# Feed-forward of a fused attention block as four f16 products on exact ternary weights, moved behind the block scores

## The reference

```
x = L0_attn_h                                                   # (2, 1024, 256)
x = _layernorm(x + _L0_attn_ref(x, ...))                        # 16 heads of 128, window of 64 + compressed blocks of 16
x = _layernorm(x + _L0_ffn_ref(x, weight, bias))

def _L0_ffn_ref(x, weight, bias):
    scale = jnp.mean(jnp.abs(weight))
    w_t = jnp.clip(jnp.round(weight / (scale + EPS)), -1.0, 1.0)
    w_ste = weight + jax.lax.stop_gradient(w_t * scale - weight)
    return jnp.einsum('bsi,oi->bso', x, w_ste) + bias
```

## Time and profile before

| | |
|---|---|
| median of 3 runs | 435.04 us (433.79 to 436.04) |
| profiled execution, its own time | 433.26 us |
| its span in the trace | 431.3 us (2.0 us lie around it) |
| mean granted TensorE clock | 0.966 of full speed |
| steps with a feed-forward and attention | i = 2 to 15, each 19.6 to 22.1 us |
| tail without attention | i = 16 and 17, from 405.2 us to the end |

### The profile page before, as it was taken

The page is one execution under the profiler, slowest core; times in us unless marked ns, Lnnn a source line. Parts: engine busy times, 40 slices in busy tenths (PEclk is TensorE's granted clock), DMA queues, the critical chain, the costliest instruction groups (busy, mean ns, idle before and its releaser), DMA issues.

```text
span 431.3 us, 8663 instructions
## 1 busy us (share of the span) xinstructions
PE 374.5 (87%) x3111; PEld 305.3 (71%) x3111; DVE 339.8 (79%) x679; ACT 275.1 (64%) x802; POOL 302.6 (70%) x190
## 2 busy tenths in 40 slices
PE   6996798688898999999898999898999999888782
PEld 5994586476676868687877786776777687767671
DVE  3686798859989999998898889999898998952411
ACT  3558845948584957667676757685958595846100
POOL 1836180538777897979797969797978888776705
PEclk9998999969999999999999999999999999999785
DMA  7992006688768597859584767685776858492330
GB/s 249 300 268 94 1 0 99 247 241 100 123 76 134 98 139 96 123 109 124 99 116 91 105 108 109 112 112 108 101 130 82 145 87 133 87 126 47 56 55 24
DMA packets 148235, 50.19 MB, mean 116 GB/s; under 512 B 136545, under 2 KB 146785, under 8 KB 147937
## 3 DMA queue, kind: packets, MB, share of 16 engines
q1 hardware_dynamic: 147376, 49.31, 64.4%
q10 hardware_dynamic: 816, 0.33, 0.3%
HBM read 11.87 MB, written 4.19 MB: 37 GB/s over the span
## 4 chain that ended last, share of the span: by engine, by line
PE 30%; DVE 20%; ACT 17%; POOL 14%; issue 11%; DMA 4%; SPq 1%; POOLq 0%; ACTq 0%; DVEq 0%
ACT room_h L816 12%; PE PS L658 8%; POOL ao L1191 6%; PE PS L609 4%; PE PS L576 4%; DVE room_wg L1090 3%; DVE ao L1090 3%; PE PS L637 3%; PE PS L427 3%; PE PS L629 3%; POOL room_wo L1235 3%; DMA aoT<-ao 2%; DVE room_K L1039 2%; DVE room_K L1104 2%; PE PS L467 2%
## 5 line engine op out<-in xcount | busy, mean ns | idle before, releaser
L1191 POOL TENSOR_TENSOR ao<-room_wg,ao 128x1024 f16<-128x1024 f32 x32 | 68.2, 2133 | 24.8 <-ACT ao L698 17.8
L658 PE MATMUL PS<-V,room_wg 128*128 128x129 f32 x512 | 69.9, 288 | 14.9 <-ACT room_h L816 8.9
L658 PEld LDWEIGHTS PS<-V,room_wg 128*128 128x128 f32 x512 | 64.7, 200 | 20.7 <-ACT room_h L816 11.3
L1201 POOL TENSOR_TENSOR room_wg<-room_comp,keep 128x1024 f32<-128x1024 f32 x32 | 74.7, 2356 | 2.0 <-ACT room_comp L807 2.0
L816 ACT ACTIVATE room_h<-PS,room_K 128x8 f32<-128x8 f32 (+7 forms) x256 | 70.4, 361 | 2.6 <-DVE room_K L1039 2.3
L816 ACT ACTIVATION_READ_ACCUMULATOR room_h<-PS,room_K 128x1 f32 x256 | 61.8, 247 | 0.0
L629 PE MATMUL PS<-Weff,aoT 128*128 128x256 f16 x512 | 58.5, 273 | 2.5 <-DMA aoT<-ao 2.4
L1207 POOL TENSOR_TENSOR ny<-nx,nu 128x16 f32<-128x16 f32 x16 | 46.8, 2923 | 18.4 <-DVE nx L1012 18.3
L629 PEld LDWEIGHTS PS<-Weff,aoT 128*128 128x128 f16 x512 | 48.9, 97 | 8.5 <-issue 2.6
L576 PE MATMUL PS<-room_h,kT 128*128 128x512 f16 x192 | 46.3, 379 | 6.9 <-DVE room_wg L1090 6.6
L803 ACT ACTIVATE room_comp<-PS 128x512 f32<-128x512 f32 x64 | 37.4, 599 | 16.1 <-PE PS L576 15.9
(11 more groups left out here) (178 smaller groups left out, 759.5 us busy)
## 6 DMA issues: line engine op xcount, KB each, us to landing
H<-in_L_attn_h SPq DMA_DIRECT2D x4, 512.0 KB, 6.3
room_wg<-in_L_attn_Wg SPq DMA_DIRECT2D x1, 2048.0 KB, 12.6
cw_rows<-staged SPq DMA_DIRECT2D x1, 2048.0 KB, 6.4
CW<-cw_rows SPq DMA_DIRECT2D x1, 2048.0 KB, 7.9
out<-room_wo SPq DMA_DIRECT2D x16, 128.0 KB, 2.6
CW<-in_L_attn_Wq_up SPq DMA_DIRECT2D x2, 512.0 KB, 12.5
room_wo<-in_L_attn_Wo SPq DMA_DIRECT2D x1, 1024.0 KB, 13.8
room_h<-room_K SPq DMA_TRANSPOSE x64, 3.2
```

What stands on the lines that cost most here:

```text
L658: last = nc.tensor.matmul(pv, Pm[:, c, 2 * pr:2 * pr + 2, :], V[:, 2 * i + c, :], start=True, stop=True)
L1191: G.tensor_tensor(ao16[:, 1, :, c, :], ao[:, c, :, :], ao16[:, 0, :, c, :], ALU.subtract).then_inc(g_al, 1)
L1201: G.tensor_tensor(Pm[:, c, :, :], E[:, c, :, :], keep[:, :, :], ALU.mult).then_inc(g_mask, 1)
```

## The change

The feed-forward's weight stays ternary (-1, 0, 1) in f16, which holds it exactly; `x1` is split into an f16 high part and an f16 rest, so the product becomes four f16 matmuls (two parts, two halves of the contraction) where there were two f32 ones. The rest is a new DVE instruction per step, `x1T[:, 1]`, and `scale` is put in afterwards, by the residual sum. On PE the feed-forward moves from between the window scores to behind the block scores, and its result from bank 7 to bank 6, which the values use next: they get a wait for z (`d_fr`), and the projection loses its own. On DVE z and its statistics move from ahead of the rotary products to behind the second half's. The new instruction stands where z stood.

```
-        wfT = sb("wfT", [P, KC, HID])
+        wfT = sb("wfT", [P, 2, KC, HID], f16)[:, 0, :, :]
...
-        x1T = part(room_h, 2048, "p (k n) -> p k n", KC * P, k=KC)
+        x1T = part(room_h, 2048, "p (x k n) -> p x k n", KC * P, x=2, k=KC).bitcast(f16)
+        ternary = part(room_h, 3584, "p (k n) -> p k n", KC * HID, k=KC)
...
+        def x1_bank(mid):
+            return (bank(7) if mid else bank(6))[:, HID:2 * HID]
         def ffn_bank(mid):
-            return bank(7) if mid else bank(6)
+            return bank(6)[:, 0:HID] if mid else bank(6)[:, HID:2 * HID]
...
                 def feed_forward():
-                    pe.wait_ge(a_xt, i - 1)
+                    pe.wait_ge(d_xl, i - 1)
                     for k in range(KC):
-                        last = nc.tensor.matmul(ffn_bank(mid)[:, HID:2 * HID], x1T[:, k, :], wfT[:, k, :],
-                                                start=k == 0, stop=k == KC - 1)
+                        for n in range(2):
+                            last = nc.tensor.matmul(ffn_bank(mid), x1T[:, n, k, :], wfT[:, k, :],
+                                                    start=k == n == 0, stop=k == KC - 1 and n == 1)
                     last.then_inc(p_f, 1)
...
-                        if ffn and u == 1:
-                            feed_forward()
...
                     last.then_inc(p_cs, 1)
+                    if ffn:
+                        pe.wait_ge(a_tanh, 4 * i + 4)
+                        feed_forward()
...
-                    if ffn and mid:
-                        pe.wait_ge(d_fr, t)
...
                     pe.wait_ge(g_mask, 2 * i + c + 1)
                     if c == 0:
                         pe.wait_ge(a_tanh, 4 * i + 4)
+                        if ffn:
+                            pe.wait_ge(d_fr, i - 1)
...
                 if ffn:
-                    dve.wait_ge(p_f, i - 1)
-                    dve.wait_ge(g_xb, i - 1)
-                    wait(dve, g_out, i - 2)
-                    V_.tensor_tensor(z[:, :], ffn_bank(mid)[:, HID:2 * HID], x1b, ALU.add).then_inc(d_fr, 1)
-                    dve.wait_ge(d_fr, i - 1)
-                    chained(V_.bn_stats(bns[:, 1, :], z[:, :]))
+                    dve.wait_ge(a_xt, i - 1)
+                    V_.tensor_tensor(x1T[:, 1, :, :], x1_bank(mid).rearrange("p (k n) -> p k n", k=KC),
+                                     x1T[:, 0, :, :], ALU.subtract).then_inc(d_xl, 1)
...
                 if front:
                     rope_products(1)
+                if ffn:
+                    dve.wait_ge(p_f, i - 1)
+                    dve.wait_ge(g_xb, i - 1)
+                    wait(dve, g_out, i - 2)
+                    V_.scalar_tensor_tensor(z[:, :], ffn_bank(mid), fscale[:, 0:1], x1b, ALU.mult,
+                                            ALU.add).then_inc(d_fr, 1)
+                    dve.wait_ge(d_fr, i - 1)
+                    chained(V_.bn_stats(bns[:, 1, :], z[:, :]))
```

More of the change, by code:

```diff
@@ L200, in build @@
         d_nq, d_nl, g_rs = sem("d_nq"), sem("d_nl"), sem("g_rs")
-        d_red, d_qn, d_rope, d_add, d_cmax, d_rc, d_ql, d_ao, d_fr, d_y, d_hi = (sem(n) for n in (
-            "d_red", "d_qn", "d_rope", "d_add", "d_cmax", "d_rc", "d_ql", "d_ao", "d_fr", "d_y", "d_hi"))
+        d_red, d_qn, d_rope, d_add, d_cmax, d_rc, d_ql, d_ao, d_fr, d_y, d_hi, d_xl = (sem(n) for n in (
+            "d_red", "d_qn", "d_rope", "d_add", "d_cmax", "d_rc", "d_ql", "d_ao", "d_fr", "d_y", "d_hi", "d_xl"))
         g_mask, g_cn, g_al, g_rl, g_x1, g_xb, g_out = (sem(n) for n in (
@@ L522, in ffn_weights @@
                         last = nc.tensor.transpose(b[:, (2 * k + o) * P:(2 * k + o + 1) * P],
-                                                   wfT[:, o, k * P:(k + 1) * P], ident[:, :])
+                                                   ternary[:, o, k * P:(k + 1) * P], ident[:, :])
                 end(last)
@@ L548, in step @@
                     for k in range(KC):
-                        last = nc.tensor.transpose(ffn_bank(mid)[:, HID + k * P:HID + (k + 1) * P],
+                        last = nc.tensor.transpose(x1_bank(mid)[:, k * P:(k + 1) * P],
                                                    x1[:, k * P:(k + 1) * P], ident[:, :])
@@ L789, in step @@
                     act.wait_ge(p_xt, i - 1)
-                    narrow(x1T[:, :, :], ffn_bank(mid)[:, HID:2 * HID].rearrange("p (k n) -> p k n", k=KC), a_xt)
+                    narrow(x1T[:, 0, :, :], x1_bank(mid).rearrange("p (k n) -> p k n", k=KC), a_xt)
                 if front:
@@ L1174, in _ @@
             G.tensor_scalar(fthn[:, :], fthr[:, :], -1.0, None, ALU.mult).then_inc(s_fth, 1)
-            G.tensor_scalar(fw_a[:, :, :], fw_s[:, :, :], fthr[:, 0:1], fscale[:, 0:1], ALU.is_gt, ALU.mult)
+            G.tensor_scalar(fw_a[:, :, :], fw_s[:, :, :], fthr[:, 0:1], 1.0, ALU.is_gt, ALU.mult)
             pool.wait_ge(s_fth, 2)
-            G.tensor_scalar(fw_b[:, :, :], fw_s[:, :, :], fthn[:, 0:1], fscale[:, 0:1], ALU.is_lt, ALU.mult).then_inc(s_fth, 1)
+            G.tensor_scalar(fw_b[:, :, :], fw_s[:, :, :], fthn[:, 0:1], 1.0, ALU.is_lt, ALU.mult).then_inc(s_fth, 1)
             pool.wait_ge(s_fth, 3)
-            G.tensor_tensor(wfT[:, :, :], fw_a[:, :, :], fw_b[:, :, :], ALU.subtract).then_inc(s_fw, 1)
+            G.tensor_tensor(ternary[:, :, :], fw_a[:, :, :], fw_b[:, :, :], ALU.subtract).then_inc(s_fw, 1)
             def step(i, front, mid, proj, ffn):
```

## The result

The changed kernel takes 423.85 us (median of 6 runs, 421.39 to 425.18), the kernel before 434.42 beside it (6 runs, 432.15 to 437.7): ratio 0.9749, 95% interval 0.970 to 0.980, so 10.6 us faster. In a second session it took 425.11 (422.91 to 427.01) against 432.81: ratio 0.9807 (0.9761 to 0.9853), 7.7 us. The forecast was a gain of 8.5 and a time of 426.5. Medians and ratios leave out executions over 1.5% above the fastest of the same kernel; with them the median of the kernel with the high part alone would be 427.4 (3.5 over the changed kernel's), and those of the two with spare transposes 423.0 and 430.85.

What follows compares the result with a forecast made beforehand. Each step lasts as long as the latest of three paths from D (exponentials, masks, DVE) to the values' last four records. Steps 8.0 plus tail 0.5 gave 8.5 off 433.26, 424.8 profiled, 426.5 median; range 423.8 to 431.5.

Steps and rivals of the forecast that it cites:

- the 8.0 for the loop: Gain summed over the steps, each the least of 0.86 and the last four value records' wait beyond D + 10.1.
- The tail: Steps 16 and 17, subtraction in line, product with half the columns: gain 0.2 and 0.3, together 0.5 us.
- the median shown is 1.8 above that run: Last term: 1.8 us from the profiled run to the median, taking 424.8 to 426.5.
- 1.19 by DVE, 0.86 by PE plus 0.25 slack: Block maximum: DVE allows 1.19 us earlier, its scores 0.86 plus 0.25 slack, so 1.07; 0.9 in large steps.
- I take 0.86 for all: Block exponentials on ACT start 0.86 to 1.0 us earlier; 0.86 was used for every step.
- could start at D + 10.1: Masks path: the values' last four records on PE could start at D + 10.1, then wait 0.91 to 1.1 for exponentials.
- the deductions of 0.3 for DVE and 0.2 for step 12: Taken off the steps' gain: 0.3 for DVE in six steps of 6 to 8 groups, 0.2 where `aoT` landed last.
- The landing hangs on D: Steps 2 and 11 gain nothing: PE waited there for `aoT`, up to 1.0 us, and its landing follows D.
- Rival 1: DVE or a landing sets the step; gain only 2.5 to 6, time 429 to 432.5, say 431; chance 0.24.
- Rival 2: Slower, DVE-bound: subtraction, larger z and waits add 0.45 per step to DVE, time 441; chance 0.07.
- Rival 3: No change: the masks bind every step, four records not before D + 11, time 435; chance 0.07.
- Rival 4: More than forecast: each long-wait step gains 1.1 in place of 0.86, 10.5 in all, time 424.5; chance 0.10.

Runs made afterwards that it cites:

- the kernel with the high part alone: Changed kernel with two f16 products of x1's high part, no low part and no subtraction on DVE: 426.59 us; with spare transposes 423.12 us.
- the two with spare transposes: Changed kernel and kernel before, each with 10 to 15 spare PE transposes at steps 15 to 17: 422.02 us and 430.38 us.
- the two half-kernels: Kernel before with z in two buffers by turns, 432.36 us; kernel before without the feed-forward product in steps 2 to 15, 432.97 us.
- the kernels with six and with 22 spare transposes: Changed kernel with 6 or 22 in place of 14 spare transposes at the very start of PE: 425.11 us and 425.41 us.
- the kernel with z in two buffers: Kernel before with z in two buffers by turns, so z need not wait for POOL's L1235: 432.36 us, ratio 0.9964.
- the one without the middle products: Kernel before without the feed-forward's matmuls in steps 2 to 15, z adding x1 instead: 432.97 us, ratio 0.9983.

## Why the prediction came out as it did

**The step that failed: the terms outside the loop.** The forecast of 426.5 stands 2.65 above the measured 423.85, and the 8.0 for the loop has no part in that. Two terms of the sum were mis-sized. The tail was put at 0.5, and the profiled pair gained 1.94 there. And "the median shown is 1.8 above that run" was carried over to the changed kernel: its profiled run took 423.94 (424.8 forecast) and its median is 423.85, so this term was -0.1. The 1.8 came from three executions; the other medians of the kernel before, 432.81 to 434.42, lie between 0.5 below and 1.2 above its profiled 433.26. Against the two stands the setup, put at nothing, which took 0.55 longer. By the second session (425.11) the forecast is 1.4 too high.

**Right: the loop.** A gain of 8.0 was forecast for the steps; 8.02 in the first profile, 8.6 in the second. Both halves' interplay was named (1.19 by DVE, 0.86 by PE plus 0.25 slack), and the two half-kernels show it.

**Right only in sum, by luck: the size per step.** The step "**0.86 to 1.0**. I take 0.86 for all" was mis-sized, and against its own terms: the least of 1.07 and 0.86 + 0.25 is 1.07. The exps ahead of the block exponentials had 0.25 of slack, so the maximum's 1.07 came through: 1.08 in step 13, and steps 12 to 14 gained 0.95, 1.07 and 0.97. In steps of 8 groups 0.85 is right (22.07 to 21.23), for there the block scores bounded the maximum already. In step 13, as in 4, 9, 10 and 12, the masks on POOL then take over as bound: the values start at D + 8.7 and the last four records at D + 10.13, as read ahead ("could start at D + 10.1"). Two landings and a transpose of queries took the surplus back: step 5 gained 0.31 and step 3 0.18 in the first profile, 0.42 and 0.70 in the second. So steps 3 to 7 gained 2.9 where 4.1 was forecast, and steps 10 and 12 to 15 4.4 where 3.9 was; the deductions of 0.3 for DVE and 0.2 for step 12 did not come. "The landing hangs on D" was the incomplete part: steps 2 and 11 did give nothing, but step 5 joined them, and with a landing in time step 2 would have gained 1.2 and step 11 0.8, as the kernels with six and with 22 spare transposes show.

**Right: DVE beside it.** Subtraction 0.41 for 0.40, z 0.48, z's stall gone, no wait of PE for z in the values. The drag of 0.05 on six steps measures 0.08 in step 13 (`divide(0)` at D + 10.96, where the records would let it start at 10.88).

**The tail.** 0.5 was forecast and 1.94 came in this pair. In the profiles, from the transposes of x1 to the product's end takes 3.21 and 3.23 in steps 16 and 17 before, and 2.45 and 2.65 after: 1.3 together. The product is 2.07 before and this after:

```profile
399.28 1.04 PE L562 MATMUL PS<-wfT,room_h 128*128 128x256 f16 x4 [1.00 <-DVE room_h L1023]
400.11 4.72 PE L616 MATMUL PS<-CW,room_wo 128*128 128x256 f32 x16
...
415.35 1.03 PE L562 MATMUL PS<-wfT,room_h 128*128 128x256 f16 x4 [0.93 <-DVE room_h L1023]
```

Halved, at one clock, and the handover through DVE adds 0.5 to the wait of 0.47. The prediction halved step 16's share; but the clock was at 0.50 there too, and the old product took 2.07 in both steps. Part of this 1.3 is the clock's all the same: the same stretches take 2.96 and 2.28 in the kernel with z in two buffers, 2.36 and 3.23 in the one without the middle products. The other 0.67 is the blocks' projection (L616), 4.72 against 5.39, and is the clock's: the low level covers 2.2 us of it against 3.6, and where it covers none (the high part alone) it takes 3.62. That part is not the change's. Over all profiles with an unchanged tail the kernel before has 26.12, 23.68 and 24.89 (mean 24.9; with z in two buffers and without the middle products), the changed one 24.18, 24.39, 25.37, 24.30 and 24.21 (mean 24.5; also with the old bank, whose tail is the same, and with 6 and 22 spare transposes): 0.4 apart, near the 0.5 of the forecast.

**The setup** was taken as unchanged and stands at 97.9 to 101.0 in the profiles of all kernels, with no order between them. It and the falls of the clock are the largest differences between profiles of like kernels: 98.55 and 99.82 in the two of the changed kernel, whose spans are 421.9 and 422.8.

**The rivals.** Rival 1 (a landing sets some steps) is true of steps 2, 5 and 11 and of no more: 1.2, 0.8 and 0.7 us by the comparisons above. Rival 2 (DVE-bound, 441) fell: DVE is busy 18.97 of 19.57 us in step 13, and adding 0.43 to it costs 0 to 0.38. With the rule of the Trainium skill (Perfetto Trace Analysis, Identifying the Most-Contended Engine) one would have relieved DVE; the trace does not agree: the kernel without the subtraction is faster in step 4 alone, by 0.2, and the one that loads DVE by 5.6 more than before is 2.5% faster. Rival 3 (no change) fell with every run. Rival 4 named the right mechanism, 1.1 in steps with long waits, and the wrong extent. Its 424.5 lies nearest to the first median, but not for its reason: the steps gave 8.0, not 10.5. The f16 form itself is worth 1.4 at most (0.1 by the second session); forecast was 0.3 to 0.5 from it in the tail and nothing in the steps.

The fastest by median is the changed kernel with spare transposes (422.02); its interval overlaps that of the changed kernel, which took 423.85 in one session and 425.11 in the other.

## What to carry to other kernels

Where two inputs of one instruction come by two engines with less than 0.3 us between them, no single cure shows: the stall in the chain of waits (11.8 us here) was worth 1.3 to 1.6 by itself, the work taken off PE nothing beyond the noise, and both together 8. Read both arrival times from the start of a step before a stall is counted as a gain, and test the halves. When work moves, look at which buffer or bank lets it: the same move with its result in the old bank cost 28 us, some 10 of them through falls of the granted clock.

## What the runs showed of the hardware

- A 16 KB packet of the instruction queue that starts 3.5 to 4.2 us after D goes with a landing of the transposing DMA 1 us late, 42 of 42 times. A late landing costs 0.8 us in step 5 (20.32 for 19.56) and 1.2 in step 2 (20.02 for 18.84).
- The granted clock falls to the 1.2 GHz level for 3.4 us at a time, at other places in each kernel: at 378 us in three kernels (step 15 22.9 for 21.2), at 124 us in one (step 2 21.69 for 20.0), at 243 us in one (in step 8), and in six steps of the kernel with the old bank. One such fall costs 1.6 to 1.7 us where PE is busy. Spare transposes in the tail did not prevent the first fall there.
- The changed kernel's median was 423.85 in one session and 425.11 in another; step lengths of undisturbed steps repeat to 0.02. For differences below 1% the steps tell more than the medians.
